# The score stage's stacked columns of tiles 0 to 11, turned by VectorE and moved through DRAM instead of by TensorE and ScalarE

## The chip, the cores and the metric

The kernel runs on one core of one Trainium2 chip. The metric is the device time of one execution in microseconds (us). The engines are TensorE (PE, with its weight loads as PEld), VectorE (DVE), ScalarE (ACT), GpSimd (POOL) and SyncE (SP), which here issues every DMA from one queue, in program order.

## What is computed

Cut to what matters, with B = 2 batches, S = 2048 rows of x, 640 columns, 8 heads of 80, a context of 128 rows of 384 (124 text rows `enc`, 4 rows `ca`):

```
query = x @ Wq;  keyt = enc @ Wk;  valt = enc @ Wv
hs      = mha(query, keyt, valt)                 # 2048 queries, 124 keys, 8 heads
ca_q1   = (ca^T @ Wq_ca)[indices]                # 2048 rows picked out of 384
ca_hs1  = mha(ca_q1, x, x)                       # the keys and values are x itself
ca_hs2  = mha(ca_hs1 @ Wq, ca @ Wk_ca, ca @ Wv_ca)
out     = (hs + ca_hs2) @ Wout + b_out + x
```

All is float32. A product is made of two or three passes over high and low halves.

## The kernel before

Each batch is 16 tiles of 128 rows of x, and goes through three stages: the score stage (of which this text is), the stage of the second attention (32 "quads"), and the output stage. The score stage of batch 0 is at about 52 to 202 us of the profile, that of batch 1 at about 396 to 547 us.

In the score stage, each tile i needs this:

- SyncE loads the tile's rows of x into one of `X_BUFS` = 3 buffers of `xin`, in 32x32 blocks, as four DMAs (L384). The first three tiles of a batch are loaded ahead of the stage.
- VectorE turns the blocks (`x_blocks`, L878, `xTr<-xin`), ScalarE rounds to `xT_hi` (L672), and VectorE makes `xT_lo` (`xT`, L884). There is one `xTr` and there are two of each half.
- TensorE makes the tile's scores in three parts, k = 0, 1, 2 (L1275), 15 matmuls each, into four slots of PSUM. Beside the scores of the heads, part 0 holds 32 columns g, and parts 1 and 2 hold columns y.
- VectorE takes the least score of each head (`least`, L892), ScalarE the exponentials into `ex` and their sums (`exps`, L691). VectorE inverts the sums (`inv`, L919, `rinv<-sums`), and GpSimd multiplies `ex` by them (`normalise`, L582, `norm_made`). SyncE then writes `ex` to DRAM (L420, `ex_kept<-ex`). VectorE takes the low half of y (`y_low`, L912).
- VectorE spreads the g columns into `gs` as high and low halves (`g`, L905 and L907). TensorE transposes `gs` by two matmuls with the identity (`g_stack`, L1233), and ScalarE copies the result from PSUM bank 5 to the tile's columns of `gT` (L705). These are the stacked columns: in each group of 32 partitions one head's slots, and the 128 rows of the tile along the free side.
- Six "units" per tile, each two matmuls of `gT` with `aTm` (L1250) and one VectorE maximum over 512 columns (L925, `mpart<-PS`), in two PSUM banks in turn.

Nothing is scheduled by a planner: each engine's instructions stand in the order of the code, and semaphores tie them. In step i of the stage TensorE makes the scores of tile i and, at fixed places among the 45 matmuls (`UNIT_AT`), three units of tile i-1, the transposes of `gs` (place 26), and three units of tile i. VectorE's step i is `least(i-1, 2)`, one unit, `x_blocks(i+1)`, `y_low`, `least(i, 0)`, `g(i)`, one unit, `xT(i+1)`, `y_low`, one unit, `inv(i-1)`, `least(i, 1)` and three units. SyncE's part of the stage is a loop in the order shown first in the section on the change: at turn i it waits for the turned blocks of tile i-1 (`xTr_made`), loads tile i+2 in its place, waits for the normalised tile i-1 (`norm_made`), and writes that.

GpSimd has other work between the first `normalise` calls: value strips (both batches), and `sel`, `wo_hi` and `wo_lo` (batch 0).

Of the kernel before, what the change touches and what calls it, by code (L numbers as in the profile page):

```python
# [49 lines left out]
HERE = 3  # L50
TURNED = 3
# [63 lines left out]
def build(nc, x, ctx_in, wq, wk, wv, wqca, wkca, wvca, wout, bout, out):  # L115
# [6 lines left out]
    with ctx:  # L122
        def sb(name, shape, dt=F32):
            return ctx.enter_context(nc.sbuf_tensor(name, shape, dt))

        def sem(name):
            return ctx.enter_context(nc.semaphore(name))
# [30 lines left out]
        gs = sb("gs", [P, 2, NH, SLOTS])  # L158
        as_ = sb("as_", [P, CT, NH, SLOTS])
# [165 lines left out]
        ex_kept = nc.dram_tensor("ex_kept", (B, TILES, P, NH * P), F32, kind="Internal").ap()  # L325
        p2_kept = nc.dram_tensor("p2_kept", (B, NH * NT, S), F32, kind="Internal").ap()
# [17 lines left out]
        gsh_made, gs_made, gT_ps, gT_made = sem("gsh_made"), sem("gs_made"), sem("gT_ps"), sem("gT_made")  # L344
        rinv_made, norm_made = sem("rinv_made"), sem("norm_made")
# [29 lines left out]
        def _(sp):  # L375
# [271 lines left out]
        def _(act):  # L647
# [18 lines left out]
            for b in range(B):  # L666
# [35 lines left out]
                def g(i):  # L702
                    T = b * TILES + i
                    act.wait_ge(gT_ps, T + 1)
                    nc.scalar.activation(gT[:, :, i * P:(i + 1) * P], PS[:, 5, P:P + SETS * P].rearrange("p (s n) -> p s n", s=SETS),  # L705
                                         ACT.Copy).then_inc(gT_made, 1)
# [6 lines left out]
                g(0)  # L713
# [4 lines left out]
                for i in range(1, TILES - 1):  # L718
                    exps(i - 1, 2)
                    xT(i + 1)  # L720
                    exps(i, 0)
                    g(i)
                    exps(i, 1)
# [90 lines left out]
        def _(dve):  # L814
# [56 lines left out]
            for b in range(B):  # L871
# [29 lines left out]
                def g(i):  # L901
                    T = b * TILES + i
                    if T >= 2:
                        dve.wait_ge(gT_ps, T - 1)
# [37 lines left out]
                xT(1)  # L942
                least(0, 1)
                for n in range(HERE):
                    unit(0, n)
# [6 lines left out]
                for i in range(1, TILES - 1):  # L952
                    least(i - 1, 2)
                    unit(i - 1, HERE)
# [204 lines left out]
        def _(pe):  # L1159
# [66 lines left out]
            for b in range(B):  # L1226
                def g_stack(i):
                    T = b * TILES + i
                    if T:
                        pe.wait_ge(gT_made, T)  # L1230
# [23 lines left out]
                UNIT_AT = {3: (-1, 3), 12: (-1, 4), 21: (-1, 5), 35: (0, 0), 39: (0, 1), 43: (0, 2)}  # L1254
                LAST_AT = {3: (-2, 3), 12: (-2, 4), 21: (-2, 5), 33: (-1, 0), 37: (-1, 1), 41: (-1, 2), 45: (-1, 3), 49: (-1, 4), 53: (-1, 5),
# [64 lines left out]
                pe.wait_ge(gT_made, (b + 1) * TILES)  # L1320
# [200 lines left out]
```

## Time and profile before

| | |
|---|---|
| median of 3 runs | 743.89 us (740.9 to 744.16) |
| the profiled execution | 743.51 us, its span in the trace 741.8 us |
| busy share of the span | PE 96%, PEld 88%, DVE 77%, ACT 50%, POOL 23% |
| DMA | 82.22 MB, mean 111 GB/s |

Times in the trace count from the start of the span. The difference between the span and the execution's own time (1.7 us) lies outside the trace. Matmuls are pipelined, so how long TensorE is held by one is read from the distance between starts, not from its duration; the same is done below for VectorE, whose neighbouring instructions overlap a little. An instruction shown on SPq is the issue of a DMA, which holds SyncE; the data lands later ("to landing" counts from the start of the issue).

### The profile page before, as it was taken

To read this page: it belongs to the slowest core of one execution; us is meant where nothing else is said; L and a number is where in the kernel's file an instruction comes from. 1 tells how busy PE (TensorE), PEld (TensorE's weight loads), DVE (VectorE), ACT (ScalarE), POOL (GpSimd) and SP (SyncE) were. 2 spreads that over 40 slices of the span, in tenths; PEclk is the share of its full clock that TensorE was granted. 3 is DMA by queue.
4 is the path that set the end of the run, shared out by engine and by line. 5 is a ranking of instruction groups with operands and counts; after the bars stand their busy time and mean duration, and the time that the engine had idled before them with its cause. 6 is when DMAs were issued, how large, how long until landed. Compare 5 with 4: busy or idle time off the path is not lost.

```text
span 741.8 us, 12206 instructions
## 1 busy us (share of the span) xinstructions
PE 713.3 (96%) x4491; PEld 653.3 (88%) x4491; DVE 573.2 (77%) x955; ACT 374.0 (50%) x942; POOL 172.6 (23%) x205
## 2 busy tenths in 40 slices
PE   7999999999899999998999999999989998999998
PEld 5978999999867778998999999999967777999997
DVE  3656888888899999776865888888899999665662
ACT  1634445544489982333333555454479996232321
POOL 8035951111200000541230511111110000322220
PEclk9999999999999999999999999999999999999999
DMA  8724253343320007899925344444230005597932
GB/s 225 225 100 116 70 125 92 93 94 93 112 68 1 1 16 144 208 206 205 237 96 106 86 97 96 93 94 93 94 133 1 1 1 113 96 246 184 189 107 75
DMA packets 232580, 82.22 MB, mean 111 GB/s; under 512 B 214524, under 2 KB 215932, under 8 KB 232520
## 3 DMA queue, kind: packets, MB, share of 16 engines
q1 hardware_dynamic: 232520, 81.43, 44.8%
q8 instruction: 36, 0.59, 0.3%
q14 instruction: 24, 0.20, 0.1%
HBM read 50.00 MB, written 31.33 MB: 110 GB/s over the span
## 4 chain that ended last, share of the span: by engine, by line
PE 67%; DVE 11%; SPq 6%; issue 6%; ACT 4%; POOL 3%; DMA 3%; DVEq 0%; ACTq 0%
PE PS L1275 28%; PE PS L1482 13%; PE PS L1250 5%; PE PS L1461 5%; SPq L443 4%; PE PS L1377 3%; DVE e_lo L1028 3%; ACT e_hi L741 3%; PE PS L1222 2%; PE PS L1347 2%; PE PS L1368 2%; DVE e_hi L1020 2%; PE PS L1185 2%; DMA exT<-p_kept 1%; POOL wo_lo L621 1%
## 5 line engine op out<-in xcount | busy, mean ns | idle before, releaser
L925 DVE TENSOR_REDUCE mpart<-PS 128x4 f32<-128x512 f32 x192 | 131.4, 686 | 36.8 <-PE PS L1250 36.4
L1275 PE MATMUL PS<-mm_hi,xT_hi 128*128 128x280 f32 (+3 forms) x480 | 159.5, 332 | 0.0
L1275 PE MATMUL PS<-mm_hi,xT_lo 128*128 128x280 f32 (+3 forms) x480 | 157.4, 328 | 0.0
L1275 PE MATMUL PS<-mm_lo,xT_hi 128*128 128x280 f32 (+3 forms) x480 | 156.5, 326 | 0.0
L630 POOL TENSOR_TENSOR xin<-xin,bias 128x640 f32<-128x640 f32 x32 | 51.2, 1605 | 309.4 <-issue 193.2
L582 POOL TENSOR_TENSOR ex<-ex,rinv 128x992 f32<-128x992 f32 x30 | 55.4, 1847 | 201.0 <-DVE rinv L919 200.9
L691 ACT ACTIVATE ex<-PS,neg 128x124 f32<-128x124 f32 x256 | 90.1, 364 | 11.7 <-DVE gs L907 6.5
L1275 PEld LDWEIGHTS PS<-mm_hi,xT_hi 128*128 128x128 f32 x480 | 90.2, 188 | 0.7 <-issue 0.5
L1275 PEld LDWEIGHTS PS<-mm_lo,xT_hi 128*128 128x128 f32 x480 | 90.4, 188 | 0.3
L1275 PEld LDWEIGHTS PS<-mm_hi,xT_lo 128*128 128x128 f32 x480 | 90.3, 188 | 0.2
L783 ACT ACTIVATE oT_hi<-PS 128x256 fp32r<-128x256 f32 x80 | 29.9, 386 | 118.1 <-PE PS L1461 111.4
L1028 DVE TENSOR_TENSOR e_lo<-e,e_hi 128x1536 fp32r<-128x1536 f32 (+1 forms) x46 | 77.1, 1688 | 4.5 <-ACT e_hi L741 3.7
L1250 PE MATMUL PS<-gT,aTm 128*128 128x256 f32 x384 | 76.8, 281 | 1.9 <-DVE mpart L925 1.3
L1482 PE MATMUL PS<-wo_hi,oT_hi 128*128 128x320 f32 x320 | 74.1, 313 | 2.0 <-DVE oT_lo L1092 1.5
L1482 PE MATMUL PS<-wo_hi,oT_lo 128*128 128x320 f32 x320 | 73.4, 311 | 0.0
L1482 PE MATMUL PS<-wo_lo,oT_hi 128*128 128x320 f32 x320 | 73.4, 311 | 0.0
L1250 PEld LDWEIGHTS PS<-gT,aTm 128*128 128x128 f32 x384 | 67.6, 188 | 3.0 <-DVE mpart L925 1.6
L681 ACT ACTIVATE ybuf<-PS 128x96 fp32r<-128x96 f32 x64 | 16.2, 254 | 105.1 <-DVE neg L892 105.1
L735 ACT ACTIVATE e<-PS 128x1536 f32<-128x1536 f32 x44 | 64.2, 1460 | 7.9 <-PE PS L1347 7.2
L1092 DVE TENSOR_TENSOR oT_lo<-PS,oT_hi 128x256 fp32r<-128x256 f32 x80 | 32.6, 418 | 44.9 <-ACT oT_hi L783 44.9
L1377 PE MATMUL PS<-e_lo,ybuf 128*98 128x384 f32 (+1 forms) x256 | 57.2, 345 | 4.5 <-DVE e_lo L1028 4.3
L1347 PE MATMUL PS<-aTs,gT 128*128 128x512 f32 x192 | 56.5, 405 | 3.9 <-DVE aTs L1003 2.2
(158 smaller groups left out, 1329.4 us busy)
## 6 DMA issues: line engine op xcount, KB each, us to landing
ex_kept<-ex SPq DMA_DIRECT2D x32, 512.0 KB, 2.9
ex<-ex_kept SPq DMA_DIRECT2D x112, 128.0 KB, 3.1
xin<-in_x SPq DMA_DIRECT2D x128, 80.0 KB, 2.9
xin<-in_x SPq DMA_DIRECT2D x32, 320.0 KB, 4.1
out<-res SPq DMA_DIRECT2D x32, 320.0 KB, 3.0
raw_kept<-raw SPq DMA_DIRECT2D x5, 512.0 KB, 3.0
ex<-ex_kept SPq DMA_DIRECT2D x4, 512.0 KB, 5.0
mm_lo<-raw_kept SPq DMA_DIRECT2D x10, 186.0 KB, 3.2
```

The lines of the kernel that those rows point to most:

```text
L582: nc.gpsimd.tensor_tensor(ex[:, i % 2, :, 0:NK], ex[:, i % 2, :, 0:NK], rinv[:, i % 2, :].unsqueeze(2).broadcast_to([P, NH, NK]), ALU.mult ...
L630: nc.gpsimd.tensor_tensor(x_slot(u), x_slot(u), bias[:, :], ALU.add).then_inc(xbias, 1)
L691: last = nc.scalar.activation(ex[:, i % 2, h, 0:NK], s_ps(T, h), ACT.Exp, bias=neg[:, i % 2, h:h + 1], scale=-1.0, accum_out=sums[:, i % 2 ...
L735: nc.scalar.activation(e_of(p), flat(sT_bank(p), 3), ACT.Exp, scale=SCALE).then_inc(e_made, 1)
L925: nc.vector.tensor_reduce(mpart[:, n // 2, :, 2 * (n % 2):2 * (n % 2) + 2, i].rearrange("p s k -> p k s"), PS[:, 6 + N % 2, :].rearrange(" ...
L1028: nc.vector.tensor_tensor(e_lo[:, p % LO_BUFS, c0:c1], e_of(p)[:, c0:c1], e_hi[:, p % HI_BUFS, c0:c1].bitcast(F32), ALU.subtract)\
L1250: last = mul(PS[:, 6 + N % 2, k * G2:(k + 1) * G2].rearrange("p (s n) -> p s n", s=SETS), aTm[:, r0 + k, c * P:(c + 1) * P], gT[:, :, i * ...
L1275: last = mul(PS[:, slot(T, k), p0:p0 + w], l[:, i % 2, j, :], rr[:, m0:m0 + w], start=(j == 0 and n == 0), stop=(n == 2), skip_group_check ...
L1347: last = mul(PS[:, sT_bank(p) + n, :], gT[:, s, kt * P:(kt + 1) * P], aTs[:, s].rearrange("p r n -> p (r n)")[:, n * BANK:(n + 1) * BANK], ...
L1377: last = mul(PS[0:y_cols(r), 6 + r // 2, 0:CAD], y_of(kt, s * R + r), e_lo[:, p % LO_BUFS, r * CAD:(r + 1) * CAD], start=False, stop=(kt = ...
L1461: last = mul(PS[:, 6 + j % 2, 0:G2], strip(vv, j, h)[0:rows], pp[0:rows, h, :], start=(n == 0 and k == 0), stop=(g > 1 and n == 2 and k + ...
L1482: last = mul(PS[:, out_bank(2 * g + u) + f, 0:HALF], l[:, j, u * P:(u + 1) * P], rr[:, j, f * HALF:(f + 1) * HALF], start=(j == 0 and n == ...
```

## The change

For tiles 0 to 11 (`MOVED` = 12) of each batch the two transposes and ScalarE's copy fall away. Instead VectorE turns the 32x32 blocks of `gs` into a new buffer `gsT` (`gs_blocks`, one for all tiles), SyncE writes it to a DRAM tensor `g_kept` by four DMAs (`move_out`), and reads it back into `gT` by four more (`move_in`). Tiles 12 to 15 go as before. The units stand about half a step later: step i now has three units of tile i-2 and three of tile i-1. Steps 12, 13 and 14 have eight each, so that the last steps end with the same work. In SyncE's loop the write stands ahead of the wait for the normalised tile, and the read stands behind the write of `ex`. The load of x, with its own wait, is now behind both.

```diff
+MOVED = 12
...
+        gsT = sb("gsT", [P, NH * SLOTS])
...
+        def units_of(i):
+
+            first = (0, 0, 3) + tuple(9 + 6 * n for n in range(10)) + (71, 79, 87)
+            return [(q // UNITS, q % UNITS) for q in range(first[i], first[i + 1])]
...
+                def move_in(i):
+
+                    sp.wait_ge(g_out[i % 2], (uses(b * TILES + i) + 1) * 64)
+                    if b and i == 0:
+                        sp.wait_ge(sT_ps, b * QUADS)
+                    rows = g_kept[b, i].rearrange("k (s r) n -> r k s n", s=SETS)
+                    for r in range(R):
+                        sp.dma_start(gT[r * SLOTS:(r + 1) * SLOTS, :, i * P:(i + 1) * P].bitcast(F32), rows[r]).then_inc(g_in[i % 2], 16)
+
+                def move_out(i):
+
+                    sp.wait_ge(gsT_made, moved(b * TILES + i) + 1)
+                    for n in range(P // SLOTS):
+                        sp.dma_start(g_kept[b, i, :, :, n * SLOTS:(n + 1) * SLOTS],
+                                     gsT[n * SLOTS:(n + 1) * SLOTS, :].rearrange("k (h t) -> k h t", h=NH)).then_inc(g_out[i % 2], 16)
                 for i in range(TILES):
                     T = b * TILES + i
                     if i >= 1:
+                        if i == 1:
+                            move_out(0)
+                            move_in(0)
+                        if i < MOVED:
+                            move_out(i)
+                        sp.wait_ge(norm_made, T)
+                        sp.dma_start(ex_kept[b, i - 1], ex[:, (i - 1) % 2].rearrange("p h k -> p (h k)")).then_inc(ex_out[(i - 1) % 2], 16)
+                        if i < MOVED:
+                            move_in(i)
                         sp.wait_ge(xTr_made, T)
                         load_x(x_use(b, 0, i - 1) + X_BUFS)
-                        sp.wait_ge(norm_made, T)
-                        sp.dma_start(ex_kept[b, i - 1], ex[:, (i - 1) % 2].rearrange("p h k -> p (h k)")).then_inc(ex_out[(i - 1) % 2], 16)
...
+                def gs_blocks(i):
+                    T = b * TILES + i
+                    dve.wait_ge(gs_made, T + 1)
+                    if moved(T):
+                        dve.wait_ge(g_out[(i - 1) % 2], ((moved(T) - 1) // 2 + 1) * 64)
+                    nc.vector.transpose(gsT[:, :], gs[:, i % 2].rearrange("p h n -> p (h n)")).then_inc(gsT_made, 1)
...
-                    if n == 0:
-                        pe.wait_ge(gT_made, b * TILES + i + 1)
+                    T = b * TILES + i
+                    if n == 0 and i < MOVED:
+                        pe.wait_ge(g_in[i % 2], (uses(T) + 1) * R * 16)
+                    elif n == 0:
+                        pe.wait_ge(gT_made, stacked(T) + 1)
...
-                        scores(i, k, 15 * k, {q: (i + d, n) for q, (d, n) in UNIT_AT.items() if i + d >= 0}, {26: i})
+                        scores(i, k, 15 * k, units_at, {26: i} if i >= MOVED else {})
```

SyncE's queue before, inside the score stage. `xin` is a tile of x, `ex` the exponentials of a tile, and the semaphore in brackets is what the row waits for:

```order
L384 DMA xin<-in_x 32x20x32 [waits xTr_made]
L384 DMA xin<-in_x 32x20x32 x3
L420 DMA ex_kept<-ex 128x1024 [waits norm_made]
L384 DMA xin<-in_x 32x20x32 [waits xTr_made]
L384 DMA xin<-in_x 32x20x32 x3
L420 DMA ex_kept<-ex 128x1024 [waits norm_made]
```

The same place of the changed kernel, one turn of the loop and the start of the next:

```order
L448 DMA g_kept<-gsT 256x1x32 [waits gsT_made]
L448 DMA g_kept<-gsT 256x1x32 x3
L459 DMA ex_kept<-ex 128x1024 [waits norm_made]
L442 DMA gT<-g_kept 32x2x128 [waits g_out0]
L442 DMA gT<-g_kept 32x2x128 x3
L405 DMA xin<-in_x 32x20x32 [waits xTr_made]
L405 DMA xin<-in_x 32x20x32 x3
L448 DMA g_kept<-gsT 256x1x32 [waits gsT_made]
```

At turn i both load tile i+2. Before, that load stood behind the write of tile i-2's `ex`; now it stands behind the write of tile i-1's `ex` and four reads of `gT`.

VectorE's order before, from the turned blocks of one tile (`x_blocks(i+1)`) to the inverse sums (`inv(i-1)`):

```order
L878 STREAM_TRANSPOSE xTr<-xin 128x640
L912 TENSOR_TENSOR ybuf<-PS,ybuf 128x2x2x24
L892 TENSOR_REDUCE neg<-PS 128x2
L905 CAST gs<-PS 128x8x8
L907 TENSOR_TENSOR gs<-PS,gs 128x8x8
L925 TENSOR_REDUCE mpart<-PS 128x2x2
L884 TENSOR_TENSOR xT_lo<-xTr,xT_hi 128x640
L912 TENSOR_TENSOR ybuf<-PS,ybuf 128x2x2x24
L925 TENSOR_REDUCE mpart<-PS 128x2x2
L919 RECIPROCAL rinv<-sums 128x8
```

The same stretch in the changed kernel:

```order
L921 STREAM_TRANSPOSE xTr<-xin 128x640
L964 TENSOR_TENSOR ybuf<-PS,ybuf 128x2x2x24
L935 TENSOR_REDUCE neg<-PS 128x2
L950 CAST gs<-PS 128x8x8
L952 TENSOR_TENSOR gs<-PS,gs 128x8x8
L977 TENSOR_REDUCE mpart<-PS 128x2x2
L959 STREAM_TRANSPOSE gsT<-gs 128x256
L927 TENSOR_TENSOR xT_lo<-xTr,xT_hi 128x640
L964 TENSOR_TENSOR ybuf<-PS,ybuf 128x2x2x24
L977 TENSOR_REDUCE mpart<-PS 128x2x2
L971 RECIPROCAL rinv<-sums 128x8
```

One transpose of 256 columns came in; the two unit maxima of the stretch are of older units than before.

## Rows read from the trace of the kernel before

**Rows 1.** The page: busy tenths of PE and the granted clock, 40 slices

```profile
PE   7999999999899999998999999999989998999998
PEclk9999999999999999999999999999999999999999
```

**Rows 2.** Windows, one step of 9.05 us: each engine's busy time, clock, DMA

```profile
119.60:128.65 9.05, 9.05 (x61) 8.96 (x60) 7.51 (x17) 4.51 (x21) 1.85 (x1) 1.00 0.40 95
```

**Rows 3.** Timeline of PE where the two transposes stand (start, duration, instruction)

```profile
121.43 0.36 PE L1275 MATMUL PS<-mm_hi,xT_lo 128*128 128x420 f32 x1
121.62 0.35 PE L1275 MATMUL PS<-mm_lo,xT_hi 128*128 128x420 f32 x1
121.81 0.38 PE L1233 MATMUL PS<-ident,gs 128*128 128x128 f32 x2
122.20 0.33 PE L1275 MATMUL PS<-mm_hi,xT_lo 128*128 128x372 f32 x1
```

**Rows 4.** Timeline of SP: two turns of its loop

```profile
124.50 0.33 SPq L420 DMA_DIRECT2D ex_kept<-ex  x1
124.86 2.92 SPq L384 DMA_DIRECT2D xin<-in_x  x4
133.54 0.33 SPq L420 DMA_DIRECT2D ex_kept<-ex  x1
```

**Rows 5.** Timeline of DVE: the later use of the tile loaded at 124.86

```profile
136.68 0.84 DVE L878 STREAM_TRANSPOSE xTr<-xin 128x640 f32<-128x640 f32 x1
```

**Rows 6.** Timeline of DVE and POOL, from one `x_blocks` to `normalise`

```profile
118.59 0.83 DVE L878 STREAM_TRANSPOSE xTr<-xin 128x640 f32<-128x640 f32 x1
...
120.26 0.68 DVE L925 TENSOR_REDUCE mpart<-PS 128x4 f32<-128x512 f32 x1
120.85 0.81 DVE L884 TENSOR_TENSOR xT_lo<-xTr,xT_hi 128x640 fp32r<-128x640 f32 x1
...
122.35 0.19 DVE L919 RECIPROCAL rinv<-sums 128x8 f32<-128x8 f32 x1
...
122.62 1.85 POOL L582 TENSOR_TENSOR ex<-ex,rinv 128x992 f32<-128x992 f32 x1 [7.20 <-DVE rinv L919]
```

**Rows 7.** VectorE's longest block transposes by line: ns min/median/max

```profile
L1076 DVE STREAM_TRANSPOSE exT<-ex x28: 1201/1244/1247, 283.6 to 707.9; 128x1024 f32<-128x1024 f32 x28
```

**Rows 8.** DMA issues by line: ns min/median/max; for x, us to landing

```profile
L384 SPq DMA_DIRECT2D xin<-in_x x128: 578/650/3571, 15.7 to 515.8; - x128
...
DMA to landing us min/median/max: 2.5/2.9/7.5
```

**Rows 9.** The same for the writes of `ex`

```profile
L420 SPq DMA_DIRECT2D ex_kept<-ex x30: 320/326/332, 70.5 to 541.0; - x30
...
DMA to landing us min/median/max: 2.8/2.9/4.4
```

**Rows 10.** The same for a load with rows of three pieces (output stage)

```profile
L500 SPq DMA_DIRECT2D mm_lo<-raw_kept x15: 469/487/1347, 320.8 to 353.3; - x15
```

**Rows 11.** Timeline of DVE: `least(0, 2)`, then `x_blocks` of tiles 3 and 15, batch 0

```profile
63.70 0.48 DVE L892 TENSOR_REDUCE neg<-PS 128x3 f32<-128x372 f32 x1
...
72.41 0.83 DVE L878 STREAM_TRANSPOSE xTr<-xin 128x640 f32<-128x640 f32 x1
...
181.92 0.84 DVE L878 STREAM_TRANSPOSE xTr<-xin 128x640 f32<-128x640 f32 x1
```

**Rows 12.** Timeline of batch 1: SP's last loads, `x_blocks` of tiles 3 and 15

```profile
399.25 5.46 SPq L384 DMA_DIRECT2D xin<-in_x  x8
...
416.88 0.83 DVE L878 STREAM_TRANSPOSE xTr<-xin 128x640 f32<-128x640 f32 x1
...
525.44 0.83 DVE L878 STREAM_TRANSPOSE xTr<-xin 128x640 f32<-128x640 f32 x1
```

**Rows 13.** Windows between the score stage and the next, batch 0 (columns as Rows 2)

```profile
200.00:203.00 3.00, 1.12 (x4) 0.60 (x4) 2.88 (x5) 2.94 (x10) 0.00 (x0) 0.97 0.22 85
203.00:206.00 3.00, 3.00 (x8) 2.25 (x9) 2.29 (x2) 2.07 (x3) 0.00 (x0) 0.50 0.54 187
```

More of the change, by code:

```diff
@@ L227, in part, with stacked, moved, uses @@
             return T // TILES * 3 * TILES + PART_AT[T % TILES, k]
+        def stacked(T):
+            return T // TILES * (TILES - MOVED) + max(T % TILES - MOVED, 0)
+        def moved(T):
+            return T // TILES * MOVED + min(T % TILES, MOVED)
+        def uses(T):
+            return T // TILES * MOVED // 2 + T % TILES // 2
+        def units_of(i):
+            first = (0, 0, 3) + tuple(9 + 6 * n for n in range(10)) + (71, 79, 87)
+            return [(q // UNITS, q % UNITS) for q in range(first[i], first[i + 1])]
         def slot(T, k):
@@ L325, in build @@
         ex_kept = nc.dram_tensor("ex_kept", (B, TILES, P, NH * P), F32, kind="Internal").ap()
+        g_kept = nc.dram_tensor("g_kept", (B, MOVED, SLOTS, NH, P), F32, kind="Internal").ap()
         p2_kept = nc.dram_tensor("p2_kept", (B, NH * NT, S), F32, kind="Internal").ap()
@@ L344, in build @@
         gsh_made, gs_made, gT_ps, gT_made = sem("gsh_made"), sem("gs_made"), sem("gT_ps"), sem("gT_made")
+        gsT_made, g_out, g_in = sem("gsT_made"), [sem("g_out0"), sem("g_out1")], [sem("g_in0"), sem("g_in1")]
         rinv_made, norm_made = sem("rinv_made"), sem("norm_made")
@@ L703, in g @@
                     T = b * TILES + i
-                    act.wait_ge(gT_ps, T + 1)
+                    act.wait_ge(gT_ps, stacked(T) + 1)
                     nc.scalar.activation(gT[:, :, i * P:(i + 1) * P], PS[:, 5, P:P + SETS * P].rearrange("p (s n) -> p s n", s=SETS),
@@ L712, in _ @@
                 exps(0, 0)
-                g(0)
                 if b:
@@ L721, in _ @@
                     exps(i, 0)
-                    g(i)
+                    if i >= MOVED:
+                        g(i)
                     exps(i, 1)
@@ L902, in g @@
                     T = b * TILES + i
-                    if T >= 2:
-                        dve.wait_ge(gT_ps, T - 1)
+                    if T >= 2 and (T - 2) % TILES < MOVED:
+                        dve.wait_ge(gsT_made, moved(T - 2) + 1)
+                    elif T >= 2:
+                        dve.wait_ge(gT_ps, stacked(T - 2) + 1)
                     nc.vector.tensor_copy(gs_half(i, 0).bitcast(F32R), g_rep(T)).then_inc(gsh_made, 1)
@@ L942, in _ @@
                 xT(1)
+                gs_blocks(0)
                 least(0, 1)
-                for n in range(HERE):
-                    unit(0, n)
                 if b == 0:
@@ L952, in _ @@
                 for i in range(1, TILES - 1):
+                    units = units_of(i)
+                    more = len(units) > UNITS
+                    a, c = (0, 0) if len(units) < UNITS else (1 + more, 4 if more else 3)
                     least(i - 1, 2)
-                    unit(i - 1, HERE)
+                    for q in units[:a]:
+                        unit(*q)
                     if i + 1 < TILES:
@@ L959, in _ @@
                     g(i)
-                    unit(i - 1, HERE + 1)
+                    for q in units[a:a + 1] if a else ():
+                        unit(*q)
+                    if i < MOVED:
+                        gs_blocks(i)
                     xT(i + 1)
                     y_low(i - 1, 2)
-                    unit(i - 1, HERE + 2)
+                    for q in units[a + 1:c] if a else ():
+                        unit(*q)
                     inv(i - 1)
                     least(i, 1)
-                    for n in range(HERE):
-                        unit(i, n)
+                    for q in units[c:]:
+                        unit(*q)
                 i = TILES - 1
@@ L1228, in g_stack @@
                     T = b * TILES + i
-                    if T:
-                        pe.wait_ge(gT_made, T)
+                    if stacked(T):
+                        pe.wait_ge(gT_made, stacked(T))
                     pe.wait_ge(gs_made, T + 1)
@@ L1252, in unit @@
                     last.then_inc(mx_ps, 1)
-                UNIT_AT = {3: (-1, 3), 12: (-1, 4), 21: (-1, 5), 35: (0, 0), 39: (0, 1), 43: (0, 2)}
-                LAST_AT = {3: (-2, 3), 12: (-2, 4), 21: (-2, 5), 33: (-1, 0), 37: (-1, 1), 41: (-1, 2), 45: (-1, 3), 49: (-1, 4), 53: (-1, 5),
+                UNIT_AT = (3, 12, 21, 35, 39, 43)
+                MORE_AT = (3, 8, 13, 23, 28, 33, 38, 43)
+                LAST_AT = {2: (-2, 1), 7: (-2, 2), 12: (-2, 3), 17: (-2, 4), 22: (-2, 5), 33: (-1, 0), 37: (-1, 1), 41: (-1, 2), 45: (-1, 3), 49: (-1, 4), 53: (-1, 5),
                            58: (0, 0), 62: (0, 1), 66: (0, 2), 70: (0, 3), 74: (0, 4), 78: (0, 5)}
@@ L1284, in step @@
                 def step(i):
+                    units = units_of(i)
+                    units_at = dict(zip(MORE_AT if len(units) > UNITS else UNIT_AT[-len(units):], units)) if units else {}
                     for k in range(3):
-                        scores(i, k, 15 * k, {q: (i + d, n) for q, (d, n) in UNIT_AT.items() if i + d >= 0}, {26: i})
+                        scores(i, k, 15 * k, units_at, {26: i} if i >= MOVED else {})
                 def last_steps():
@@ L1319, in _ @@
                 last_steps()
-                pe.wait_ge(gT_made, (b + 1) * TILES)
+                pe.wait_ge(gT_made, (b + 1) * (TILES - MOVED))
                 pe.wait_ge(asm_made, b + 1)
```

## The prediction

> **What bounds the kernel now.** I read the page first: TensorE is busy in nine tenths or more of nearly every slice, and its clock is fully granted [rows 1]. A busy TensorE is not by itself the bound, so I looked at one step of the score stage by windows: in 9.05 us TensorE has no idle time, while VectorE is busy 7.51 and GpSimd 1.85 [rows 2]. The steps repeat at this length (x_blocks of tile 3 to tile 15 takes 109.51 us in batch 0 and 108.56 in batch 1, twelve steps each [rows 11, 12]). So in this stage whatever TensorE is relieved of would be gained, until another chain closes at nearly the same length.
>
> Then I read SyncE's timeline, because the change puts eight more DMAs and a new order into its only queue. The load issued from 124.86 on is that of tile i+2 in the turn that follows the write at 124.50 [rows 4]. Its four issues end at 127.78; the last begins near 127.1 and lands 2.9 later [rows 8], at about 130.0. VectorE takes that tile at 136.68 [rows 5]. **The load has 6.7 us to spare, less than one step.**
>
> **What is removed.** On TensorE two transposes for each of 24 tiles. From the matmul at 121.62 to the second one behind the transposes, at 122.20, are 0.58 us [rows 3]. Two score matmuls alone take 0.36 (0.19 for 420 columns, read from 121.43 to 121.62, and 0.17 for 372). So the pair holds TensorE for 0.22 us, and 24 pairs for 5.3 us. ScalarE loses one copy per tile, worth nothing here: it is busy 4.51 of 9.05 [rows 2].
>
> **What is added on VectorE.** One block transpose of 256 columns per moved tile. The trace has 640 columns at 0.83 [rows 6] and 1024 at 1.244 [rows 7], so 1.07 ns a column and 0.15 fixed: 0.42 for 256, of which about 0.07 overlaps the next instruction, as at the other instructions. I take 0.35. VectorE has 9.05 - 7.51 = 1.54 us free per step [rows 2], so this alone hides: 7.9 of a step that would last 8.83.
>
> **What is moved.** At turn i SyncE loads tile i+2. Before, that waited only for the normalised tile i-2. Now it stands behind the wait for the normalised tile i-1, the write of its ex, the wait for four writes of g_kept, and four reads. At the old pace, normalise ends one step later (write of ex at 133.54 [rows 4]). Reads and loads follow, and the tile that was there at 130.0 would be there at about 140.9 for a use at 136.68. It is late in every step, and VectorE stands still at x_blocks, with all units, minima and the next inverse sums queued behind it. That closes a ring, since x_blocks(i+1) must run before inv(i-1), which releases the load for x_blocks(i+2):
>
> - x_blocks to rinv 3.76 (118.59 to 122.35 [rows 6]), plus 0.35 for the new transpose: 4.11
> - rinv to the start of normalise 0.27, normalise 1.85, to the issue of ex 0.03 (122.62 + 1.85 to 124.50 [rows 4, 6]): 2.15
> - the write's issue, start to start, 0.36 (124.50 to 124.86)
> - four reads. No such DMA is in the trace. A 128-row copy is issued in 0.33 [rows 9], a load of three short pieces per row in 0.49 [rows 10], one of twenty pieces in 0.65 [rows 8]. Reads have two pieces per row; I take 0.49, nearest in shape: 2.0. Bounds 0.33 and 0.65 give 1.3 and 2.6.
> - three issues of x ahead of the last one, at 0.70: 2.1; landing 2.9 (2.5 at least) [rows 8]
>
> The ring is **13.6 us** in place of 9.05. I checked the wait on g_out inside it: gs_blocks ends 2.26 + 0.42 = 2.68 after x_blocks (118.59 to 120.85, plus its own duration [rows 6]), the fourth write begins 1.5 later and lands after about 2.9, the median of the writes of ex [rows 9], at 7.1. The reads could begin at 6.6. A write of 32 KB should land sooner than one of 512 KB, so I cost this at 0; with 2.9 it is 0.5, with the longest landing of ex (4.4) and issues of 0.65 it is 2.5.
>
> TensorE is hidden inside: while VectorE stands still it ends parts 0 and 1 of the tile and stops at part 2, whose slot waits for y_low. It has some 9 us of work in 13.6.
>
> **Sum.** Ten rings of 13.6 per batch carry tiles 4 to 13. Tiles 14 and 15 have neither reads nor gs_blocks: 13.6 - 2.35 = 11.3. From tile 3 to 15 that is 158.6, against 109.5 and 108.6: **+49.1 and +50.0.**
>
> Tile 3 is late too, since its load was free of any normalise before. Batch 0: least(0, 2) at 63.70 is released by a clearing that doesn't change, x_blocks(2) follows 0.4 later, rinv 2.9 after that (3.76 + 0.35, less two unit maxima of 0.60 that stand elsewhere), normalise ends at 69.1. The writes of g land at 70.6; four reads, three x issues and the landing lead to 77.6, against 72.41 [rows 11]: **+5.2.** Batch 1: SyncE is busy with old loads to 404.7 [rows 12]. move_out(0) then lands at 409.1 and move_in(0) holds the queue to 411.1. The second writes land at 415.5, the reads end at 417.5, and x is there at 422.5, against 416.88: **+5.6.** GpSimd's strips and wo halves, which hold up tiles 3 and 4 of batch 0 now, fit into the longer rings.
>
> Behind tile 15 one more unit is left for VectorE, 0.6 per batch. The 5.3 us that TensorE saves go to nothing, since it waits anyway. In all 49.1 + 50.0 + 5.2 + 5.6 + 1.2 = 111.1 on the profiled execution's 743.5: **855 us.** That execution is 0.4 below the median of 743.9, which is nothing here.
>
> **One rule of the skill beside it.** What the trace says of idleness and clock: TensorE was busy for 1.12 of 3 us, and in the next 3 us its granted clock was 0.50, the 1.2 GHz level [rows 13]. The Trainium skill, TensorE: Matmul & The Clock Gate, section HAM oscillation, describes matmul bursts between DMA waits that start at half the clock each time. By that rule every ring here starts cold, and the trace agrees for the one gap above. I price it as a rival below, from rows.
>
> **Rivals.**
> *The ring closes in time, and TensorE's saving is kept.* It needs the ring below the 8.83 us of TensorE's new step, that is 4.8 us less than I get. For it speaks only that SyncE is mostly idle. Against it: 6.26 of the ring are rows up to the issue of ex, and the x issues and landing at their shortest (3 x 0.62 + 2.5) with the issue of ex (0.36) already make 11.0 without any read. Then 743.5 - 5.3 = 738. Chance 0.03, a third of it for a saving partly eaten up, within 0.5% of before.
> *The queue slips once, not in each step.* If a load could use time in which VectorE works on buffered tiles, three xin buffers would absorb the delay, leaving some 10 us per batch: 764. Against it: the load of tile i+2 needs norm(i-1), which needs x_blocks(i+1); no third buffer helps. Chance 0.04.
> *The clock.* If the half clock after each stop lasts through the step, TensorE's 8.8 us become 17.6 and it is the bound again, 4.0 more than the ring in 20 rings: 935. If it lasts for only part of the step, it fits into the idle time (13.6 - 8.8 = 4.8 us) and costs nothing. Batch 1 has the same kind of gap; the page shows a full clock in all slices [rows 1], so falls are brief. Chance 0.04.
> *The new DMAs are dear.* Issues of 0.65 and late writes: the ring is 13.6 + 0.6 + 2.5 = 16.7, 22 times 3.1 more than mine: 923. The landing of small writes would have to be far above that of large ones. Chance 0.06 for above 890.
> *VectorE becomes the bound* doesn't arise: 7.9 us against 8.83, or against 13.6.
>
> **How the numbers follow.** The forecast mechanism gets 0.83. Its cheap end is a ring of 12.2 (reads at 0.33, x issues at 0.60, landing 2.5): 1.4 less in 22 rings, and 0.7 in the four short ones: 821. Halfway to the dear end is 889. The range is 821 to 889; above and below lie the rivals and what I mis-sized inside the mechanism. A measurement of this kernel can tell about 0.5% from no change, so: faster 0.02, same 0.01, slower 0.97.
>
> **What would show it.** Right: x_blocks idle for DMA xin in each step from tile 3 on, by 4 to 5 us; steps of 13 to 14 us, about 11 for the last two; the chain of waits going VectorE, GpSimd, SyncE's issues, the landing of x, VectorE; PE below 85% busy; second attention and output stages unchanged. Wrong: x_blocks not waiting for a DMA, TensorE's steps at 8.8; or a wait on g_out or on g_in as the last to end; or a granted clock near 0.5 with TensorE busy throughout.

## The result, and the profile after

The changed kernel takes 867.19 us (median of 4 runs, 864.89 to 869.13) against 742.54 before (median of four runs, one more than in the table above): the ratio is 1.169, with a 95% interval of 1.166 to 1.172. The profiled execution is the slowest of the four, 869.13 us with a span of 867.4, so 125.6 us more span than before. Forecast were 855 us in a range of 821 to 889, or 111.1 us more.

The page of the changed kernel, busy tenths of TensorE and the clock in 40 slices, and below them the chain of waits with its shares of the span:

```profile
PE   8997686867898999998999877778698999999998
PEclk9998888798899999999999989797999999999999
...
PE 35%; SPq 21%; DMA 16%; DVE 15%; issue 9%; ACT 3%; POOL 1%; DVEq 0%; ACTq 0%
PE PS L1547 13%; DMA xin<-in_x 8%; SPq L442 7%; SPq L405 6%; PE PS L1526 6%; DMA g_kept<-gsT 5%; SPq L448 5%; PE PS L1338 3%; DVE e_lo L1087 3%; DVE xTr L921 3%; PE PS L1442 3%; SPq L486 2%; ACT e_hi L784 2%; PE PS L1281 2%; PE PS L1412 2%
```

TensorE, nine tenths busy before nearly throughout [rows 1], is at six to eight in the two score stages and as before elsewhere. SyncE's issues and the DMAs now hold 37% of the chain, and the score matmuls (L1338) are down to 3%. Before they had 9% and 28% (L1275):

```profile
PE 67%; DVE 11%; SPq 6%; issue 6%; ACT 4%; POOL 3%; DMA 3%; DVEq 0%; ACTq 0%
```

TensorE is busy for 87% of the span, 757.2 us against 713.3 before, although it has less to do: a score matmul lasts 361 ns on average and lasted 332, because part of them run at the lower clock, as shown below.

VectorE's timeline, from one `x_blocks` to the next but one (a row's bracket is the idle time before it and what ended it):

```profile
149.44 0.84 DVE L921 STREAM_TRANSPOSE xTr<-xin 128x640 f32<-128x640 f32 x1 [6.16 <-DMA xin<-in_x]
...
151.66 0.43 DVE L959 STREAM_TRANSPOSE gsT<-gs 128x256 f32<-128x256 f32 x1
152.02 0.78 DVE L927 TENSOR_TENSOR xT_lo<-xTr,xT_hi 128x640 fp32r<-128x640 f32 x1
...
153.49 0.19 DVE L971 RECIPROCAL rinv<-sums 128x8 f32<-128x8 f32 x1
...
164.33 0.84 DVE L921 STREAM_TRANSPOSE xTr<-xin 128x640 f32<-128x640 f32 x1 [6.99 <-DMA xin<-in_x]
178.33 0.84 DVE L921 STREAM_TRANSPOSE xTr<-xin 128x640 f32<-128x640 f32 x1 [5.06 <-DMA xin<-in_x]
```

SyncE's timeline in the same two turns:

```profile
152.12 2.52 SPq L448 DMA_DIRECT2D g_kept<-gsT  x4
155.62 0.33 SPq L459 DMA_DIRECT2D ex_kept<-ex  x1
156.01 2.48 SPq L442 DMA_DIRECT2D gT<-g_kept  x4
158.54 3.62 SPq L405 DMA_DIRECT2D xin<-in_x  x4
167.01 2.52 SPq L448 DMA_DIRECT2D g_kept<-gsT  x4
170.51 0.33 SPq L459 DMA_DIRECT2D ex_kept<-ex  x1
170.89 2.50 SPq L442 DMA_DIRECT2D gT<-g_kept  x4
173.43 2.67 SPq L405 DMA_DIRECT2D xin<-in_x  x4
```

Before, the tile had landed some 6.7 us ahead of its use [rows 4, 5]; now VectorE waits 4.9 to 7.8 us for it in each of the ten steps from tile 3 to tile 13 of both batches. The step from 164.33 to 178.33 is 14.0 us. The write of `ex` is issued 6.18 after `x_blocks` (`rinv` comes after 4.05, as read in the step ahead, and the write 2.13 later), the reads are issued from 6.56 on and the load of x from 9.10 on, and the tile is used at 14.0. The step ahead of it is 14.9 us: its four x issues took 3.62 in place of 2.67, because the first one lasted 1.55 instead of 0.60.

SyncE's DMAs by line, ns of issue and us to landing, min/median/max. The first pair is the writes of g, the second the reads, the third the loads of x:

```profile
L448 SPq DMA_DIRECT2D g_kept<-gsT x96: 567/609/2045, 54.9 to 617.8; - x96
...
DMA to landing us min/median/max: 1.9/2.0/3.7
...
L442 SPq DMA_DIRECT2D gT<-g_kept x96: 552/595/1674, 60.0 to 621.6; - x96
...
DMA to landing us min/median/max: 2.0/2.2/4.0
...
L405 SPq DMA_DIRECT2D xin<-in_x x128: 578/648/4847, 16.1 to 646.4; - x128
...
DMA to landing us min/median/max: 2.3/2.6/7.1
```

A DMA of 32 KB in 256 or 64 pieces holds SyncE for as long as one of 80 KB in 640 pieces [rows 8]. It does land sooner.

Windows across a stop of TensorE (busy time of PE, PEld, DVE, ACT, POOL, then the granted clock):

```profile
157.00:160.00 3.00, 3.00 (x22) 2.98 (x21) 0.34 (x1) 1.06 (x7) 0.00 (x0) 1.00 0.44 143
160.00:164.00 4.00, 1.15 (x7) 0.83 (x5) 0.00 (x0) 0.00 (x0) 0.00 (x0) 1.00 0.52 82
164.00:167.00 3.00, 1.63 (x5) 1.61 (x6) 2.63 (x8) 1.54 (x5) 0.00 (x0) 0.55 0.00 0
167.00:170.00 3.00, 3.00 (x12) 2.96 (x11) 2.63 (x7) 1.00 (x6) 1.36 (x1) 0.50 0.20 33
170.00:173.00 3.00, 3.00 (x19) 2.96 (x19) 2.10 (x4) 0.59 (x4) 0.48 (x1) 0.81 0.56 199
173.00:176.00 3.00, 3.00 (x21) 2.98 (x20) 0.27 (x1) 0.99 (x6) 0.00 (x0) 1.00 0.37 72
```

TensorE ends its work at 161, and stands for 4.2 us. When it goes on, it runs at 0.50 (1.2 GHz) for some 6 us. The next stop, which ends at 179.4, lasted 2.3 us, and behind it the clock stayed where it was:

```profile
176.00:178.00 2.00, 1.08 (x6) 0.76 (x5) 0.00 (x0) 0.00 (x0) 0.00 (x0) 1.00 0.65 102
...
180.00:182.00 2.00, 1.92 (x10) 1.26 (x9) 2.00 (x6) 0.80 (x4) 0.00 (x0) 1.00 0.00 0
```

Of the 22 stops in the rings of the two batches, 20 were followed by a stretch at 0.50. The other two are the shortest, 2.2 and 2.3 us; the 20 lasted 2.5 to 5.5 us.

### The profile page after: what moved, and what is told of

It reads as the page before. It is cut to its first block, busy times and chain, and to the rows that moved or that the text cites. A ratio compares the mean times of both kernels' runs of the same rounds, so it can differ in the third digit from the quotient of the medians.

```text
span 867.4 us, 12302 instructions
## 1 busy us (share of the span) xinstructions
PE 757.2 (87%) x4443; PEld 683.6 (79%) x4443; DVE 572.5 (66%) x979; ACT 364.2 (42%) x918; POOL 170.7 (20%) x205
## 4 chain that ended last, share of the span: by engine, by line
PE 35%; SPq 21%; DMA 16%; DVE 15%; issue 9%; ACT 3%; POOL 1%; DVEq 0%; ACTq 0%
PE PS L1547 13%; DMA xin<-in_x 8%; SPq L442 7%; SPq L405 6%; PE PS L1526 6%; DMA g_kept<-gsT 5%; SPq L448 5%; PE PS L1338 3%; DVE e_lo L1087 3%; DVE xTr L921 3%; PE PS L1442 3%; SPq L486 2%; ACT e_hi L784 2%; PE PS L1281 2%; PE PS L1412 2%
## 5 line engine op out<-in xcount | busy, mean ns | idle before, releaser
L1338 PE MATMUL PS<-mm_hi,xT_hi 128*128 128x280 f32 (+3 forms) x480 | 173.4, 361 | 70.5 <-DVE ybuf L964 70.5
L1338 PE MATMUL PS<-mm_hi,xT_lo 128*128 128x280 f32 (+3 forms) x480 | 169.4, 353 | 0.0
L1338 PE MATMUL PS<-mm_lo,xT_hi 128*128 128x280 f32 (+3 forms) x480 | 168.0, 350 | 0.0
L1338 PEld LDWEIGHTS PS<-mm_hi,xT_hi 128*128 128x128 f32 x480 | 100.2, 209 | 77.8 <-DVE ybuf L964 76.9
L977 DVE TENSOR_REDUCE mpart<-PS 128x4 f32<-128x512 f32 x192 | 129.5, 684 | 17.2 <-PE PS L1312 16.3
L921 DVE STREAM_TRANSPOSE xTr<-xin 128x640 f32<-128x640 f32 x32 | 27.0, 843 | 142.3 <-DMA xin<-in_x 142.3
L1338 PEld LDWEIGHTS PS<-mm_hi,xT_lo 128*128 128x128 f32 x480 | 99.5, 207 | 0.3
L1338 PEld LDWEIGHTS PS<-mm_lo,xT_hi 128*128 128x128 f32 x480 | 99.2, 207 | 0.6
L715 ACT ACTIVATE xT_hi<-xTr 128x640 fp32r<-128x640 f32 x32 | 23.6, 738 | 168.6 <-DVE xTr L921 168.6
L1312 PE MATMUL PS<-gT,aTm 128*128 128x256 f32 x384 | 86.9, 311 | 6.4 <-DVE mpart L977 5.8
L1312 PEld LDWEIGHTS PS<-gT,aTm 128*128 128x128 f32 x384 | 75.6, 215 | 14.8 <-DVE mpart L977 9.7
L826 ACT ACTIVATE oT_hi<-PS 128x256 fp32r<-128x256 f32 x80 | 29.9, 386 | 119.6 <-PE PS L1526 112.8
```

What stands on the lines that cost most here:

```text
L921: nc.vector.transpose(xTr[:, :], x_slot(u)).then_inc(xTr_made, 1)
L977: nc.vector.tensor_reduce(mpart[:, n // 2, :, 2 * (n % 2):2 * (n % 2) + 2, i].rearrange("p s k -> p k s"), PS[:, 6 + N % 2, :].rearrange(" ...
L1312: last = mul(PS[:, 6 + N % 2, k * G2:(k + 1) * G2].rearrange("p (s n) -> p s n", s=SETS), aTm[:, r0 + k, c * P:(c + 1) * P], gT[:, :, i * ...
L1338: last = mul(PS[:, slot(T, k), p0:p0 + w], l[:, i % 2, j, :], rr[:, m0:m0 + w], start=(j == 0 and n == 0), stop=(n == 2), skip_group_check ...
```

## The experiments

Each run has its own comparison with the kernel before on the same chip, whose medians there were 741.9 to 742.4 us. "Ring" is the chain that the prediction named: x_blocks, rinv, normalise, SyncE's issues, landing of x, next x_blocks.

**1. Load of x first (`e1_x_first`).**

```diff
                     if i >= 1:
+                        sp.wait_ge(xTr_made, T)
+                        load_x(x_use(b, 0, i - 1) + X_BUFS)
                         if i == 1:
                             move_out(0)
                             move_in(0)
...
-                        sp.wait_ge(xTr_made, T)
-                        load_x(x_use(b, 0, i - 1) + X_BUFS)
```

> The changed kernel with one thing put back: in SyncE's loop the load of x, with its own wait, stands first in the turn again, ahead of the writes of g, the norm wait and the reads. All else of the change stays. Ring theory (the load of x behind the norm wait, the write landing and the four reads closes a ring of 14.2 us per tile): the ring is opened, every one of the 125 us comes back, and TensorE's saving of 0.22 us in 24 tiles shows: 738 us, at most 743 if SyncE's own work per tile (four writes 2.55, their landing 2.0, four reads 2.5, four x issues 2.7: 9.8 less what overlaps) makes it late towards tile 12. Traffic theory (eight more small DMAs per tile slow the x loads and writes wherever they stand): stays above 850. VectorE theory (the block transpose and the later units fill VectorE): stays well above 760.

Measured: 762.23 us, ratio 1.029 (1.024 to 1.033). Of the 125 us, 105 are gone, with every added DMA and instruction in place: the order of the queue caused them. Traffic and VectorE theories fall. But my number fell as well: I had 743 at most, and 20 us against the kernel before are left. The chain of waits of this run, 119.6 to 129.5 us (start, duration, what):

```profile
119.60 0.65 SPq L448
...
120.29 0.61 SPq L448
...
120.94 0.62 SPq L448
...
121.60 1.95 DMA g_kept<-gsT
123.57 0.57 SPq L442
...
126.09 0.60 SPq L405
...
128.81 0.65 SPq L448
```

SyncE's own turn closes on itself, in 9.21 us: 2.0 to the start of the last write, 1.95 until it has landed, 2.52 for four reads, 2.72 for four loads. TensorE needs 8.83, the kernel before 9.05. The turns that follow are 9.84 and 9.20, and TensorE waits for `gT` (7.9 us in 8 waits in batch 0), ScalarE for the late writes of `ex` (13.3 us in 8 waits). TensorE has no idle time left from 526.6 to 543, behind its last wait for `gT` in batch 1: of the 19 us by which the span is longer than before, 11 are what the steps ahead of tiles 13 and 14 take beyond 9.05 (10.70 and 11.35 us in batch 0, 11.46 and 13.77 in batch 1). That fits units which waited for late reads and are made up for there.

**2. Load of x between the write of ex and the reads (`e2_x_before_reads`).**

```diff
                         sp.dma_start(ex_kept[b, i - 1], ...)
+                        sp.wait_ge(xTr_made, T)
+                        load_x(x_use(b, 0, i - 1) + X_BUFS)
                         if i < MOVED:
                             move_in(i)
-                        sp.wait_ge(xTr_made, T)
-                        load_x(x_use(b, 0, i - 1) + X_BUFS)
```

> The changed kernel with the load of x ahead of the four reads, still behind the norm wait and the write of ex. Ring theory: the ring keeps x_blocks to the issue of ex (6.6 in the trace of after), then three x issues 2.0 and the landing 2.7, so 11.3 us, the length that the last two tiles of each batch show already. 22 rings get shorter by 2.9 (batch 0 14.4, batch 1 14.0, to 11.3): about 867 - 64 = 803 us. Traffic theory: the same DMAs run, so about 867.

Measured: 812.97 us in one run. The forecast was 803, so 10 us are missing from the sum: from x_blocks of tile 3 (74.78) to tile 13 (192.98) a ring is 11.8 us, 0.5 above it. So 54 us go when only the reads and their wait for the writes of g no longer stand ahead of the load, and 51 more in experiment 1, when the norm wait and the writes don't either.

**3. The old kernel with that order alone (`e3_old_x_behind`).**

```diff
-                        sp.wait_ge(xTr_made, T)
-                        load_x(x_use(b, 0, i - 1) + X_BUFS)
                         sp.wait_ge(norm_made, T)
                         sp.dma_start(ex_kept[b, i - 1], ...)
+                        sp.wait_ge(xTr_made, T)
+                        load_x(x_use(b, 0, i - 1) + X_BUFS)
```

> The kernel before, with nothing of the change but the order: the load of x stands behind the norm wait and the write of ex. No DMA, no block transpose is added, TensorE's transposes stay. Ring theory: 3.76 + 2.15 + 0.36 + 2.1 + 2.6 to 2.9 = 11.0 to 11.3 per tile in place of 9.05, in 12 steps of each batch, plus 2 to 3 us for tile 3 of each: 743 + 50 to 58 = 793 to 801 us. Traffic or VectorE theory: 743 us, since neither is touched.

Measured: 805.3 us in one run, 4 above the upper end of the forecast. Two moved lines, with nothing added, cost 63 us. VectorE's timeline shows the same wait as in the changed kernel:

```profile
144.36 0.84 DVE L878 STREAM_TRANSPOSE xTr<-xin 128x640 f32<-128x640 f32 x1 [4.14 <-DMA xin<-in_x]
155.59 0.84 DVE L878 STREAM_TRANSPOSE xTr<-xin 128x640 f32<-128x640 f32 x1 [3.40 <-DMA xin<-in_x]
168.44 0.84 DVE L878 STREAM_TRANSPOSE xTr<-xin 128x640 f32<-128x640 f32 x1 [3.50 <-DMA xin<-in_x]
```

Of the 24 steps behind tile 3, 14 are 10.9 to 11.3 us, as worked out; the others are 11.5 to 12.9. In that from 155.59 SyncE's four x issues took 3.84 us, where the shortest four take 2.79. Over the 24 steps such issues add some 6 us, enough for what this run has above its sum; the second run has them too.

**4. Two reads in place of four (`e4_two_reads`).** The diff leaves out the matching edits of the writes and of VectorE's transpose.

```diff
-        g_kept = nc.dram_tensor("g_kept", (B, MOVED, SLOTS, NH, P), ...)
+        g_kept = nc.dram_tensor("g_kept", (B, MOVED, P, SETS * P), ...)
...
-                    rows = g_kept[b, i].rearrange("k (s r) n -> r k s n", s=SETS)
-                    for r in range(R):
-                        sp.dma_start(gT[r * SLOTS:(r + 1) * SLOTS, :, i * P:(i + 1) * P].bitcast(F32), rows[r]).then_inc(g_in[i % 2], 16)
+                    rows = g_kept[b, i].rearrange("p (n s t) -> s p n t", n=P // SLOTS, s=SETS)
+                    for s in range(SETS):
+                        sp.dma_start(gT[:, s, i * P:(i + 1) * P].bitcast(F32).rearrange("p (n t) -> p n t", n=P // SLOTS), rows[s]).then_inc(g_in[i % 2], 16)
```

> The changed kernel with the columns kept in DRAM in another order, so that two reads of 128 partitions bring them back in place of four of 32 (the same bytes, now in pieces of 128 B; the four writes have pieces of 256 B). Ring theory, by which what counts of the reads is how long their issues hold SyncE ahead of the load of x: two issues of 0.63 fewer in each of 22 rings, so 867 - 28 = 839 us, if an issue of the new shape takes as long. If what counts is bytes or pieces, the time stays or rises.

Measured: 839.09 us in one run. That it is the forecast number to the tenth is luck, since runs of the changed kernel lie up to 4 us apart. The reads bring the same bytes in more pieces, and the time is 28 us less: what counts is how long SyncE is held. (The writes changed too: their four issues take 1.73 in place of 2.52. By the next experiment a shorter branch of the writes gains nothing.)

**5. Two of the four writes from ScalarE's queue (`e9_split_writes`).**

```diff
-                    for n in range(P // SLOTS):
+                    for n in range(P // SLOTS // 2):
...
+                def move_out(i):
+
+                    act.wait_ge(gsT_made, moved(b * TILES + i) + 1)
+                    for n in (2, 3):
+                        nc.scalar.dma_start(g_kept[b, i, :, :, n * SLOTS:(n + 1) * SLOTS], ...).then_inc(g_out[i % 2], 16)
```

> The changed kernel with two of the four writes issued from ScalarE's queue, at the place where its copy of gT stood, so that they are issued beside SyncE's two. The chain of waits of after names the writes and their landing (10% of the span) on the path, but by the same trace the issue of ex, behind normalise, ends at 155.98 and the writes' landing at 156.01: two branches of equal length. Tie theory: making only the writes' branch about 1.0 us shorter leaves the ring at about 14.2, so 865 to 869 us, plus or minus what ScalarE's 1.2 us per tile does, which has idle time. If the listed chain alone set the ring, 22 x 1.0 less: 845 us.

Measured: 864.76 us in one run, at the lower end of the runs of the changed kernel (864.89 to 869.13). So the writes and their landing, which have 10% of its chain of waits, were worth nothing that can be told. In this run they are no longer among the larger parts of the chain, and GpSimd has 5% of it in place of 1%:

```profile
PE 35%; DVE 19%; SPq 17%; DMA 12%; issue 9%; POOL 5%; ACT 3%; DVEq 0%; ACTq 0%
```

The queue waits of the changed kernel agree (who waited for whom, us in total, times, longest, from 60 to 250 us):

```profile
SPq L459 <- POOL ex L625: 25.4, 12, 8.3
SPq L442 <- DMA g_kept<-gsT: 5.2, 3, 2.5
```

The reads had to wait for the writes beyond GpSimd's branch in 3 turns only. In the others the two branches end together: in the step read above the issue of `ex` ends at 155.95, the last write has landed at 156.0, and the reads start at 156.01.

**6. TensorE kept busy in the stop (`e5_warm`).**

```diff
+                            if k == 2 and 3 <= i < 12:
+                                for _ in range(18):
+                                    mul(PS[:, 5, :], mm_hi[:, 0:P], mm_hi[:, 0:BANK], start=True, stop=True, skip_group_check=True)
                             pe.wait_ge(yl_made, 2 * (b0 * TILES + i0) + k0)
```

> The changed kernel with 18 matmuls of 512 columns more, in each step from tile 3 to tile 11, into a PSUM bank that nobody reads in these steps, at the place where TensorE stops for the score slot (part 2). At 2.4 GHz they take 3.9 us, inside the 4 to 5 us in which it stands still. In the changed kernel the granted clock falls to 0.50 after each stop and is back only some 6 us later; busy in the stop, TensorE should keep it. Ring theory: the clock costs nothing in the rings, since TensorE has idle time in each, so 866 to 868 us with a granted clock near 1 in the stage. Clock theory (part of the 14.2 us is TensorE at half speed, a unit that VectorE waits for): several us faster, up to 22 x 0.5 = 11 us, so 856.

Measured: 872.05 us, ratio 1.176 (1.173 to 1.178). Windows as above:

```profile
160.00:163.00 3.00, 3.00 (x20) 2.98 (x19) 0.00 (x0) 0.61 (x4) 0.00 (x0) 1.00 0.40 126
163.00:166.00 3.00, 3.00 (x15) 2.59 (x15) 0.00 (x0) 0.00 (x0) 0.00 (x0) 1.00 0.66 103
166.00:169.00 3.00, 3.00 (x16) 2.44 (x15) 2.61 (x8) 1.54 (x5) 0.00 (x0) 1.00 0.00 0
```

The clock stayed at 1.00 there (0.984 over the span, against 0.939), and nothing was gained: the falls follow from the stops, and what they cost is hidden in the rings. Forecast were 866 to 868 us. Why it is some 5 us slower than the changed kernel stays open.

**7. TensorE's saving alone (`e6_no_turns`).** An edit of the kernel before (waits follow it).

```diff
                 def g_stack(i):
                     T = b * TILES + i
+                    if 0 < i < 12:
+                        return
```

> The kernel before with TensorE's transposes of gs left out for tiles 1 to 11 of each batch and nothing in their place (ScalarE copies the bank as it stands, so the second attention of these tiles is computed from tile 0's columns). It measures the term 'removed' by itself: 0.22 us in 22 tiles, 4.8 us, where TensorE bounds the stage, so 737 us. If something else closes at 9.05 too, or TensorE's early tiles are held by GpSimd anyway, less: 739 to 742.

Measured: 738.4 us, ratio 0.9954 (0.9936 to 0.9972), so 3.4 us less of 4.8 (2.1 to 4.7 by the interval).

**8. VectorE's block transposes alone (`e7_blocks_too`).** `gs_blocks(i)` goes into the kernel before at the changed kernel's places, without the wait on `g_out`.

```diff
                     unit(i - 1, HERE + 1)
+                    gs_blocks(i)
                     xT(i + 1)
```

> The kernel before with VectorE's block transposes of gs added for tiles 0 to 11 of each batch, into a buffer that nobody reads. It measures the term 'added on VectorE': 0.35 us in a step with 1.54 idle, so no change that can be told (within 0.3%). If VectorE's place in the step matters although it has idle time (the score slots and the unit banks wait for it in order), up to 24 x 0.35 = 8 us slower.

Measured: 742.36 us, ratio 1.0013 (0.9994 to 1.0032): no change.

**9. x first and two reads (`e8_x_first_two_reads`).** The diffs of 1 and 4 together.

> The changed kernel with the load of x first in the turn, and two reads of 128 partitions in place of four of 32. With x first alone SyncE's own turn was the bound: four writes (2.0 to the start of the last), its landing 1.96, four reads 2.52, four x issues 2.72, together 9.2 and at times 9.8 us, where TensorE needs 8.83. Queue theory: two read issues of 0.63 fewer make the turn 7.9 to 8.5, under TensorE's 8.83; steps of 8.83 throughout, 24 x 0.22 saved against the kernel before, less what the late start of each batch costs (2 us, tile 3): 738 to 744 us. Rival: the rest of the change (units half a step later, eight units in steps 12 to 14, more work bunched at the end of the stage) costs by itself; then the steps up to tile 12 are at 8.83, but the time stays several us above 744.

Measured: 741.99 us, ratio 0.9998 (0.9967 to 1.0028). SyncE's and VectorE's timelines:

```profile
125.03 0.34 SPq L461 DMA_DIRECT2D ex_kept<-ex  x1
125.41 1.33 SPq L442 DMA_DIRECT2D gT<-g_kept  x2
126.78 2.76 SPq L405 DMA_DIRECT2D xin<-in_x  x4
130.36 1.73 SPq L448 DMA_DIRECT2D g_kept<-gsT  x4
...
98.53 0.83 DVE L921 STREAM_TRANSPOSE xTr<-xin 128x640 f32<-128x640 f32 x1
109.96 0.84 DVE L921 STREAM_TRANSPOSE xTr<-xin 128x640 f32<-128x640 f32 x1
118.80 0.84 DVE L921 STREAM_TRANSPOSE xTr<-xin 128x640 f32<-128x640 f32 x1
127.63 0.84 DVE L921 STREAM_TRANSPOSE xTr<-xin 128x640 f32<-128x640 f32 x1
```

SyncE has idle time again, and the steps are 8.83: TensorE bounds them. The saving is given back, above all in two places. One step of batch 0 takes 11.43, where TensorE waits 2.3 us for reads that stand behind GpSimd's late `normalise` of tile 3 (9.93 in the kernel before). And from x_blocks(12) to the first matmul behind the last wait of the stage 49.9 us pass in each batch, against 48.1.

**10. The new order of the units alone (`e11_units_only`).**

```diff
-MOVED = 12
+MOVED = 0
...
-                        if i == 1:
-                            move_out(0)
-                            move_in(0)
+                        sp.wait_ge(xTr_made, T)
+                        load_x(x_use(b, 0, i - 1) + X_BUFS)
...
-                        sp.wait_ge(xTr_made, T)
-                        load_x(x_use(b, 0, i - 1) + X_BUFS)
```

(With them `gs_blocks(0)` goes, and ScalarE's `g(0)` comes back.)

> Only the new order of the units: the changed kernel with no tile moved (all transposes on TensorE and copies on ScalarE, no block transposes, no DMAs of g) and the load of x first, so the kernel before but for units half a step later, eight in steps 12 to 14. It measures what the change costs at the end of the stage, where the runs with steps of 8.83 us gave back 1.8 us per batch from tile 12 on. If that is the order of the units: 743 + 2 to 4 = 744 to 746 us. If it comes from the moved columns themselves (late reads): 742 to 743.

Measured: 745.5 us, ratio 1.0051 (1.0030 to 1.0072). In batch 1 the last three steps are 9.83, 9.50 and 9.36 us instead of 9.05: this is what the end of the stage gives back.

**11. Reads ahead of the norm wait too (`e10_reads_ahead`).** The ninth kernel with one more move:

```diff
                         if i < MOVED:
                             move_out(i)
+                            move_in(i)
                         sp.wait_ge(norm_made, T)
                         sp.dma_start(ex_kept[b, i - 1], ...)
-                        if i < MOVED:
-                            move_in(i)
```

> The kernel with the load of x first and two reads, and now the reads of g ahead of the norm wait too, directly behind the writes. In the run without this, one step of batch 0 took 11.4 us (9.9 in the kernel before): TensorE waited 2.3 us for gT, whose reads stood behind the normalised tile 3, which GpSimd delivers late (its wo halves). Queue theory: this wait goes, 1.5 to 2.3 us less than that run, so 739.5 to 740.5 us, 0.3% under the kernel before. If ScalarE's wait for the write of ex in the same place takes over (3.0 us in the kernel before), nothing changes: 742.

Measured: 739.73 us (12 runs), ratio 0.9959 (0.9941 to 0.9977), so 0.4% faster than the kernel before. The interval overlaps that of the ninth kernel (0.9967 to 1.0028), so the step from that one to this is not clear of noise by itself. TensorE's wait for `gT` in batch 0's held step fell from 2.3 to 0.8 us.

## Why the prediction was right, point by point

The mechanism was the forecast one, and its sum of 111.1 was 14.5 us short of the span's 125.6. Its terms, from VectorE's `x_blocks` (before: [rows 11, 12]; after: tile 3 at 77.57 and 486.42, tile 15 at 244.32 and 649.40). Tile 3 of batch 1 is counted from `x_blocks` of tile 1 (399.28 before, 465.17 after), and "behind tile 15" ends with the matmul behind the last wait of the stage:

| term | forecast | measured |
|---|---|---|
| tile 3 late, batch 0 | +5.2 | +5.2 |
| tile 3 to 15, batch 0 | +49.1 | +57.2 |
| tile 3 late, batch 1 | +5.6 | +3.7 |
| tile 3 to 15, batch 1 | +50.0 | +54.4 |
| behind tile 15, both | +1.2 | +2.3 |
| elsewhere | 0 | +2.8 |

Of "elsewhere", 2.0 us lie between the score stage of batch 0 and that of batch 1, which were to stay unchanged, and 1.1 in batch 1 ahead of tile 1, whose load is waited for longer; what follows batch 1's score stage is 0.2 shorter.

- **What bounds the kernel.** TensorE, with other chains close behind. Experiments 7 and 9 confirm it: relieved, the stage goes at 8.83. The 0.22 us per pair held in the steps; of 4.8 us, 3.4 reached the end.
- **The moved load.** Right, and shown from both sides: restored in 1, alone in 3. VectorE's new work costs nothing by itself (experiment 8). The added DMAs do cost with the load in time: 20 us in experiment 1, by SyncE's own turn.
- **The ring.** Forecast 13.6, measured 14.4 in batch 0 and 14.0 in batch 1 (tiles 3 to 13), and 11.3 as forecast for tiles 14 and 15. The mis-sized term is "four reads, 2.0". I took 0.49 us an issue from the load of three pieces per row [rows 10] as nearest in shape. They took 0.595 and a gap of 0.04, in all 2.53, near the end that I had as the upper bound. x landed in 2.8, for 2.9. That makes 14.0, and so 8 of the 12.5 us by which the steps from tile 3 to 15 exceed the sum; the rest are for the most part single issues of 1.2 to 1.6 us in place of 0.6. They were in the trace of before as a maximum [rows 8], and I used medians alone.
- **The wait on g_out**, costed at 0. Right, but as a tie: the writes landed in 2.0, at the same moment at which GpSimd's branch ended, and experiment 5 took two of them off SyncE's queue without effect. So the profile's chain goes through the writes and not through GpSimd as forecast, and on its face it shows one of the signs named for being wrong, a wait on g_out as the last to end.
- **VectorE, 0.35.** Right: 0.36 from 151.66 to 152.02, and nothing in experiment 8.
- **Behind tile 15.** Too low. I counted one unit more, 0.6; the three longer steps ahead of it belong to the same bunching. In the changed kernel the rings hid those. Experiment 10 measures the whole at 3.1 us between the medians (0.3 to 0.7% by the interval).
- **The other signs.** TensorE was to be below 85% busy and is at 87%, for the matmuls at the lower clock. VectorE was to wait 4 to 5 us for x and waits 4.9 to 7.8.
- **The clock rival.** The clock fell to 0.50 behind 20 of the 22 stops, and was back at 1.00 within the same ring. The Trainium skill, TensorE: Matmul & The Clock Gate, section HAM oscillation, has it fall at every wait for a DMA; the trace agrees for the 20 and not for the two shortest stops, so not every ring "starts cold", as the prediction took from it. The rival's price did not come: TensorE stood for 2.2 to 5.5 us in each ring even so, and experiment 6 shows that a full clock gives nothing back.
- **The rival that the queue slips once.** It failed, as all steps up to tile 15 show. But the reason given, that no third buffer helps, holds for the three there are: turn i loads tile i-1+`X_BUFS`. With a fourth buffer the same turn would bring the tile after, and the ring would span two steps, by the dependency that the prediction names. No run tested this.
- **The rival that the new DMAs are dear.** Half of it came: an issue with its gap took 0.635, for 0.65. The other half did not, since the writes landed in 2.0.
- **The rival that the saving is kept** failed where I had costed it, at the ring. With the ring open there was a second one that I had costed nowhere: SyncE's own turn, 9.21 us.

## What to carry to other kernels

When a DMA is moved in a queue, write down the wait that is now ahead of it and ask whether that wait depends on the data that the DMA brings; if so, the whole ring becomes the step, as long as it spans one step only; the three buffers of this kernel did not absorb it. Then add up all that the queue issues in one step, landings that it waits for included, against the step of the bounding engine: here eight small DMAs made a queue that looked idle the second bound. And a share in the chain of waits is not a gain: where two branches end together, shortening the one that is listed gives nothing, as in experiment 5.

## What the runs showed of the hardware

An issue cost SyncE 0.6 us for 32 KB in 64 or 256 pieces as well as for 80 KB in 640, but 0.33 for 512 KB in 128 rows [rows 9]. With the writes of g in 128 pieces of 256 B in place of 256 of 128 B, at the same bytes, it fell from 0.61 to 0.43 (medians, changed kernel and experiment 4). So the bytes don't set it, and neither does the number of pieces alone; which part of the shape does was not isolated. The Trainium skill, DMA: Bandwidth & Descriptors, section "Issuing engines are not separate DMA queues", calls the sequencer's time for a DMA usually small beside the DMA. For these small ones the runs don't agree: 0.6 us stand beside 2.0 to 2.6 from issue to landing. In the first experiment it was 8.4 us of issues per tile, of which the write of `ex` lay in the wait for a landing, where TensorE needs 8.83. Single issues of the same shape last 1.2 us and more, up to 4.8; what sets them was not found.
